# A scatter of message sums on GpSimd: one counter increment taken out of each row of the loop, and the first choice of first occurrences placed earlier

## What is computed

```python
h = relu(layernorm(x))
msg = relu(concat([h[dst], edge_attr]) @ W1a + b1a) @ W1b + b1b
summed = segment_sum(msg, src, 6250); counts = segment_sum(1, src, 6250)
agg = summed / max(counts, 1)
out = x + relu(concat([h, agg]) @ W2a + b2a) @ W2b + b2b
```

## Time and profile before

| | |
|---|---|
| median of 3 runs | 1582.05 us (1580.42 to 1586.08) |
| the profiled execution's own time | 1573.92 us |
| its span (first to last instruction) | 1572.1 us |
| busy: PE / DVE / POOL / ACT | 1464.4 / 1416.5 / 1211.8 / 1027.7 us |
| scatters on POOL (L524) | 726, 1159.3 us busy, 1597 ns mean, 308.6 us idle before them |
| granted TensorE clock over the span | 0.975 |

### The profile page before, as it was taken

One profiled execution on the slowest core, in us unless ns is written; L12 is line 12 of the kernel. 1 busy time (PEld: TensorE's weight loads), 2 busy tenths in 40 slices (PEclk: granted clock), 3 DMA queues, 4 the chain that ended last, 5 costly groups with the idle time before them and its releaser, 6 DMA issues. The chain is left out here.

```text
span 1572.1 us, 76959 instructions
## 1 busy us (share of the span) xinstructions
PE 1464.4 (93%) x31106; PEld 1397.7 (89%) x31106; DVE 1416.5 (90%) x4756; ACT 1027.7 (65%) x2192; POOL 1211.8 (77%) x803
## 2 busy tenths in 40 slices
PE   3579999999999999999999999999999999999937
PEld 2369999999999999999999999999999999999935
DVE  8868999989999999999999899999999999999937
ACT  5276667767676666676776666666667766676405
POOL 4378878788787787877888887778878888878764
PEclk8698999999999999999999999999999999999978
DMA  5776676766766667667666666766767667666533
GB/s 167 265 148 102 110 126 111 126 108 108 128 110 118 110 111 119 110 110 126 110 122 111 115 113 109 120 112 111 125 105 126 111 112 118 115 120 111 91 64 119
DMA packets 278965, 186.86 MB, mean 119 GB/s; under 512 B 190359, under 2 KB 274836, under 8 KB 277841
## 3 DMA queue, kind: packets, MB, share of 16 engines
q1 hardware_dynamic: 173630, 152.60, 38.8%
q0 software_dynamic: 104976, 29.30, 26.3%
HBM read 147.60 MB, written 34.18 MB: 116 GB/s over the span
## 5 line engine op out<-in xcount | busy, mean ns | idle before, releaser
L524 POOL DMA_INDIRECT sums<-vv,sidx x726 | 1159.3, 1597 | 308.6 <-issue 168.2
L1255 PE MATMUL rank_ps<-area 128*128 128x64 bf16 (+1 forms) x21000 | 764.9, 193 | 8.5 <-issue 2.2
L1255 PEld LDWEIGHTS rank_ps<-area 128*128 128x128 bf16 x21000 | 729.4, 98 | 29.7 <-issue 16.5
L703 ACT ACTIVATE area<-rank_ps 64x392 bf16<-64x392 f32 x1400 | 685.1, 489 | 82.3 <-PE rank_ps L1241 60.1
L951 DVE TENSOR_SCALAR area<-iota,local 128x640 bf16<-128x640 int16 x1400 | 482.6, 408 | 4.9
L1241 PE MATMUL rank_ps<-r_d,oh 128*128 128x196 bf16 x4200 | 482.0, 249 | 2.7 <-ACT area L703 2.2
L1241 PEld LDWEIGHTS rank_ps<-r_d,oh 128*128 128x128 bf16 x4200 | 345.0, 97 | 16.6 <-ACT area L703 4.0
L936 DVE TENSOR_SCALAR oh<-iota,rank 128x640 bf16<-128x640 int16 x846 | 285.0, 403 | 0.0
L686 ACT ACTIVATE r_d<-z_ps 128x384 f32<-128x384 f32 x423 | 207.9, 491 | 85.6 <-PE z_ps L1211 72.3
L691 ACT ACTIVATE vv<-c_ps 128x396 f32<-128x396 f32 x121 | 60.7, 501 | 241.1 <-PE c_ps L1230 213.5
L958 DVE TENSOR_TENSOR dense<-rank_ps,dense 128x325 f32<-128x325 f32 x280 | 136.5, 488 | 80.2 <-PE rank_ps L1255 79.5
(11 more groups left out here) (130 smaller groups left out, 721.5 us busy)
## 6 DMA issues: line engine op xcount, KB each, us to landing
ids_s<-ids SPq DMA_DIRECT2D x246, 192.0 KB
et_d<-in_e_t SPq DMA_DIRECT2D x143, 192.0 KB
ids_d<-ids SPq DMA_DIRECT2D x143, 192.0 KB
et_s<-in_e_t SPq DMA_DIRECT2D x123, 192.0 KB
sums<-vv,sidx POOLq DMA_INDIRECT x726
sums<-dense POOLq DMA_DIRECT2D x3, 1657.5 KB
wp_d<-p_table SPq DMA_DIRECT2D x286, 15.8 KB
wp_s<-p_table SPq DMA_DIRECT2D x246, 15.8 KB
```

Of the source, the lines that this page charges most:

```text
L524: nc.gpsimd.indirect_dma_start(out=sums[t][:, :], out_offset=bass.IndirectOffsetOnAxis(ap=index, axis=0), in_=rows, in_offset=None, comput ...
L703: ins = nc.scalar.activation(routed[on, t.div(MACRO).mod(2), first:second + 1:second - first, t.mod(MACRO), :], bank[on, :, :], ACT.Copy)
L1255: ins = nc.tensor.matmul(l2_ps[h][:, u * W:u * W + w], oh2[:, g, u * P:(u + 1) * P], rows[:, PARTS[r]:PARTS[r] + w], start=g % MACRO == 0 ...
```

## The change

In `scatter` the increment between the wait for the landing and the scatter goes. In the cycles of `fast`, `pick_first` is left out of the first one; that call stands in the prologue instead, between the one-hots of dense group 1 and the rank sum. The other branch (`general`, for edge lists that do not fit) is not run here and keeps its own increment.

```diff
@@ scatter, gpsimd
                         pool.wait_ge(scattered[t], before.times(16, 16))
-                        pool.sem_inc(pool_past, 1)
                         scatter_rows(k, t, sidx[:, slot, k:k + 1], vv[:, slot, k, 0:W])
                     pool.sem_inc(groups_ended, 1)
@@ fast, vector: the cycle
                         if sums_too:
                             nodes(now, 1)
-                        if n:
+                        if n and s.base:
                             pick_first(s)
@@ fast, vector: ahead of the cycles
                     hot(S, Count(1))
                     hot(DN, Count(1))
+                    pick_first(Count(0))
                     step(nc.vector.tensor_tensor(pos, pos, place, ALU.add))
                     slots_known()
                     slots(Count(0))
```

## The result

The changed kernel takes 1565.81 us (median of 5 runs, 1561.02 to 1568.94), the kernel before 1580.42 us beside it (5 runs, 1578.29 to 1586.08). The ratio is 0.990 [0.987, 0.993]: 14.6 us faster, against the 5.4 us of the forecast. The profiled executions took 1561.02 and 1573.92 us, 12.9 us apart.

A forecast was written before the change was run, and what follows sets the result against it. PE was taken to pace the middle, POOL to end the loop. 3.4 (opening) + 0.6 (group 113) + 1.4 (tail) = 5.4 us off the profiled 1573.92, so 1568.5; timed 1576.6 us from 1582.05, range 1565 to 1584.

The forecast's parts named there:

- PE sets the pace of the middle: Middle of the loop: PE, busy 198.0 of 200 us, sets the pace; POOL just keeps up.
- part 1's saving: POOL's late gaps, increment removed: 22 us of capacity (0 to 56), of which 2.0 us counts, from group 113 on.
- rival A: Whole loop: POOL is the bound in timed runs, 8 us plus the 5.4, so 1566 to 1570 us; chance 0.18.
- Part 1, the late landing: POOL's late scatters: start 0.38 us after the landing in place of 0.72, at most 0.35 us back each.
- Where the wait is kept: POOL's sequencer: a scatter's wait goes to a queue, leaving the sequencer free, so it reaches the group counter earlier.
- Rival C: POOL's scatters: the sequencer holds back a scatter with a wait as before; 1580 to 1583 us; chance 0.16.
- the tail: Scatters after group 113: six late gaps, 3.4 us over the floor, of which 1.4 us comes back.
- The lag: Group 113: POOL starts 0.91 us after the indices in place of 1.55, 0.6 us gained.
- Rival B: Between scatters: the 0.30 us belongs to the increment, 14 us at most in the tail; 1566 or so; chance 0.06.
- The net of the opening: PE's opening through group 4: 7.6 us back, less 2.4 (hole) and 1.8 (clock), net 3.4 us (1.6 to 5.2).
- the full case: PE's opening: the clock's rise put off some 10 us, costing 3.6 us; half, 1.8 us, was taken.
- Rival D: Opening cycles: PE's hole at 81.5 us leaves the clock low through them; 1584 to 1591 us; chance 0.14.

The follow-up runs named there:

- part 2 alone: The changed kernel with the increment put back between wait and scatter, group 0's choice still ahead of the rank sum: 1580.02 us, ratio 0.999.
- increments first: The changed kernel with all 726 increments back, each ahead of the waits of its tile: 1564.99 us, ratio 0.991.
- thinning: The changed kernel without the sixth scatter of each of groups 0 to 112: 1554.66 us, ratio 0.984.
- part 1 alone: The kernel before without the increment in front of the scatters, pick_first where it was: 1566.47 us, ratio 0.990.
- the shorter lag: The kernel before with LAG 1 in place of 2, scatters allowed one group further behind: 1581.39 us, ratio 1.001.

## Why the prediction was wrong

**The step that failed** is "So PE sets the pace of the middle and POOL keeps up with nothing to spare", and with it that part 1's saving "is POOL's capacity, and PE's pace uses up most of it". I had priced the saving over the late gaps at 22 us and then let only 2.0 us of it count. In its place the runs show that POOL's chain, by way of the group counter, held PE back in the middle of ordinary executions of the kernel before: 3 and 11 waits of ACT there, 8.3 and 27.6 us, in the two at 1582.58 and 1588.36 us. Taking that stop away without making POOL faster gained nothing (1.001, POOL 10.5 us behind at group 113). Taking scatters away gained 1.5% before the change and 0.7% after it, moving scatters into the body gained nothing before and 0.8% after, and half the increments gave about half the gain. The term of the sum that was wrong is the middle: I had put it at nothing, and it is 6.1 us even between the two profiled executions.

This is rival A in its mechanism, to which I gave 0.18. That its figure also comes close is luck. It adds the 8 us between the profiled run and the median to the 5.4, 13.4 us in all, where 14.6 were measured. By that sum the two profiled executions should lie 5.4 us apart, and they lie 12.9 apart; and the changed kernel's median is 4.8 us above its own profiled execution, so the 8 us did not go away as a whole.

**How the rows misled.** PE's 198.0 us of 200 is true, but of one stretch of one execution, and that execution of 1573.92 us was the fastest of the four of this kernel then at hand (1580.42 to 1586.08 the others). The sign of a bound is not PE's busy share but who waits for whom, and with a counter that lets POOL run two groups behind, such waits show only once the slack is used up. In the profiled execution it was just enough in the middle. In two further ones it was not always: a middle of 1291.8 and 1297.3 us instead of 1284.1, with 8.3 and 27.6 us of ACT's waits in it. I had said that the 8 us up to the median came "without a row on where"; the row was the earlier trace rows, in which 719 of 726 scatters come after an issue or a landing and none after the first waits for its indices. (One rest of 1.4 us at group 91 stands there as a landing, so "no rest" was nearly true.) A stream that hardly rests from its first to its last instruction, and ends last, has to be taken as a bound, even when another one is at 99%.

**Part 1, the late landing.** The price of a late landing was right in kind and low in both sizes. Wait to start was to fall from 0.72 to 0.38 us; it fell from 0.77 to 0.27. The 0.30 us between scatters does not add to a carried wait: the two overlap. So 0.50 us comes back for each late landing. On the tiles 1 to 5 of the groups, whose only wait is the landing, the gaps over 0.32 us fell from 71 with 42.7 us over the floor to 31 with 14.4 us: 28 us, where I took 22 for all tiles. Of the 71, 35 were less than 0.50 us over the floor.

**Where the wait is kept.** Here the forecast was wrong, although its sum does not hang on it: "the sequencer no longer stands at each landing" is not what the traces show. The increment of the group counter (L539, in the changed kernel L538) stands right behind the sixth scatter, so it tells when the sequencer is past that scatter. In the changed kernel no recorded update of the landing that the sixth scatter waits for comes after the counter, in any of the 121 groups; the counter follows it by 0.03 us or more. Where that scatter is late (10 times), the counter comes 0.23 us ahead of the scatter's start, and 0.03 us behind the landing in nine of the ten. In the kernel before the same two times are 0.22 and 0.54 us (22 late ones). So with the wait on the scatter, the sequencer still stands until the landing; what falls away is 0.51 us between the landing and the moment when it is past the scatter. What fills these 0.51 us behind an increment is not shown. The counter as a whole comes 1.55 us (median) ahead of the sixth scatter's start, against 0.97 us before, which is these 0.51 us and little more.

On this "DMA: Bandwidth & Descriptors" of the Trainium skill, section "Anatomy of one DMA — SWDGE (gpsimd) path", says that any semaphore wait of a DMA happens on the issuing sequencer before dispatch. The traces agree with that (0.03 us, and never earlier). What I had taken from it, that the change then brings 17 ns and no more, does not follow from it and did not come: increments ahead of the waits gave 0.991, increments behind them 0.999 (the latter with part 2 alone). "Perfetto Trace Analysis" of the Trainium skill, section "DMA Instruction — SWDGE (GPSIMD)", has the sequencer free behind a wait that stands in a queue; no run shows an instruction of POOL's sequencer that passes a waiting scatter. **Rival C** was right that the sequencer is held and wrong in its price: the start came 0.50 us earlier all the same.

**Group 113 and the tail.** The lag was to lose 0.6 us by a start 0.91 us after the indices; it lost 1.3, as the start came 0.27 us after. The tail (48 scatters) was to lose 1.4 us and lost 0.7. One of its scatters runs beside DVE's bias add and took 5.03 us for 4.26 before; without these 0.8 us the tail would be at the forecast's 1.4.

**Rival B**, the floor of 0.30 us owed to the increment, is refuted: 0.30 us in every kernel without it.

**Part 2 and PE's opening.** Nearly as forecast: PE's hole 2.39 us (2.4), the scatter of group 1 at 93.71 (92.9 or later), no stall at group 4, the clock back to 1.00 by 90 us. The first scatter came at 80.53 instead of 80.0: its indices were ready at 79.84, 0.7 us later than priced (79.15), since the rows themselves were there at 79.31 and not at 78.64, and the start took 0.69 us from there (0.91 before). The net of the opening was 2.7 us for 3.4 forecast. The clock stayed low 7.5 us longer than before, nearer to what I had set as the full case (10 us) than to the half that I took, so PE must have got back a little more elsewhere, which no run separates. That is one execution: in the profiled ones of part 2 alone and of the increments first, with holes of 2.39 and 3.19 us, the clock was low for 6.8 and 3.4 us there (85.3 to 92.1 and 82.8 to 86.2). For the time none of it matters: part 1 without part 2 gives the same 0.990, part 2 by itself 0.999. **Rival D**, the clock low over several cycles, did not come: there was one such stretch.

**What would show it.** The late starts are under 0.45 us, the late gaps lost over 20 us (28 on the tiles 1 to 5), the wait at group 4 is gone, POOL now waits for `sidx` after cycles without a sparse group: each came. The last I had named as the sign that the middle is PE's. By the same sign the middle before was not, as no row for it stands in the earlier trace rows beside the first scatter's; in the execution at 1582.58 us there were 4 such rests, in the one at 1588.36 us two, of 1.6 us in all. The forecast was to be wrong if the last scatter started earlier than 1509: it started at 1507.57.

**Where the gain stops.** After the change POOL no longer holds PE back in the middle (no wait of ACT for the counter, 12 rests of POOL), and thinning brings only 0.7% more. The tail after group 113 is still POOL's, which is why moving two sparse groups forward brings another 0.8%.

**What stays open.** Among executions in which ACT hardly waited for POOL, the middle still took 1278.0 us (the change), 1282.4 (part 1 alone), 1282.9 (increments first) and 1287.3 (the shorter lag), and with scatters left out 1271.2 and 1273.7; none of the runs separates what makes these few us, and with them the 6.1 us of the middle between the two profiled executions, in neither of which ACT waits for POOL there. And POOL's chain, from its first start to its last end, became 9.1 us shorter (1437.7 to 1428.6) although 17.2 us of rest came in, so its own time shrank by some 26 us. The median gains 14.6 us; how that comes out of the 26 was measured only as a whole.

## What to carry to other kernels

Read a bound from who rests and who waits, not from the busy share: a queue that hardly rests from first to last has to be taken as a bound, even with a busy share of 77%, and one profiled execution that is faster than all other timed ones may be the one in which the slack just held. Take a second profile before you price a stream's gain at nothing. In a queue of dependent DMAs, let nothing stand between the wait and the DMA: put counters and other instructions of the sequencer ahead of the wait. And after a change that speeds up one stream, look again at how work is divided along the loop: an edit that gained nothing before (1.002) gained 0.8% after.

## What the runs showed of the hardware

- A wait carried by a sequencer's increment in front of a scatter cost 0.50 us more than one carried by the scatter: 0.77 against 0.27 us from landing to start. Beforehand only the 0.72 us from the increment to the scatter could be read the earlier trace rows.
- That latency and the 0.30 us between two scatters overlap: POOL's next scatter starts at the later of the two, not at their sum.
- A scatter that waits held up the sequencer's next instruction in either form: the increment behind it came 0.03 us after the landing where the scatter carried the wait, 0.54 us after it where an increment carried it, and never before it.
- A scatter of 1.55 us that runs beside DVE's two-input add over 128x3328 (3.56 us) took 3.3 to 5.1 us in eleven traces, and in each it ended 1.41 to 1.43 us after the add's end, so it was held until the add was over. One that had started 0.2 us or more ahead of the add took its usual 1.55 us. POOL's other scatters in the tail took 1.54 to 1.8 us.
- In the opening of the changed kernel, with PE's rest of 2.39 us, TensorE's clock was at 1.2 GHz for 7.5 us more, with PE busy for 7.27 of the 10 us from 80 to 90; from 117 to 122 us PE was busy for less (3.23 of 5 us) at 2.4 GHz, after a stretch without a rest of that length. With the shorter lag the clock was at 1.2 GHz from 114.9 to 121.8 us after rests of 0.84 us at most.
